# Finer rounding ladders in a quantised feed-forward layer and a fourth slope term in an attention layer

## The reference, cut to what matters

```python
# attention 0: 16 heads of 64, T = 2048, d = 1024
scores = einsum('bhqd,bhkd->bhqk', q, k) / scale
bias = -dist * slopes[:, None, None]            # slopes 2 ** (-8 h / 16)
attn = softmax(where(causal_mask, -inf, bias) + scores)
out = einsum('bhqk,bhkd->bhqd', attn, v) @ Wo.T
...
# feed-forward 1: 1024 -> 4096 -> 1024
def activation_quant(x):
    scale = 127.0 / clip(max(abs(x), axis=-1), EPS_Q, None)
    return clip(round(x * scale), -128, 127) / scale
def bitlinear(x, norm_w, w):                    # rmsnorm, quantise, product
    x_q = activation_quant(rmsnorm(x, norm_w))
    return einsum('bsd,hd->bsh', x_q, weight_quant(w))
h = bitlinear(x, norm1_w, w1)                   # x_q has 1024 columns
h = act_scale * square(relu(h)) + act_bias
y = bitlinear(h, norm2_w, w2)                   # x_q has 4096 columns
```

## Time and profile before

| what | value |
|---|---|
| time, median of 3 runs | 22603.05 us (22590.02 to 22631.4) |
| the profiled execution's own time | 22617.48 us |
| its span, slowest core (6) | 22615.7 us |
| spans of the 8 cores | 22516.5 to 22615.7 us |
| busy TensorE / VectorE / ScalarE | 7728.4 / 4516.8 / 6436.2 us (34% / 20% / 28%) |
| mean granted TensorE clock, core 6 | 0.543 |

### The profile page before, as it was taken

One profiled execution on the slowest core, in us unless ns is written; L12 is line 12 of the kernel. 1 busy time (PEld: TensorE's weight loads), 2 busy tenths in 40 slices (PEclk: granted clock), 3 DMA queues, 4 the chain that ended last, 5 costly groups with the idle time before them and its releaser, 6 DMA issues.

```text
span 22615.7 us, 119266 instructions; the slowest of 8 cores (22516.5 to 22615.7 us)
## 1 busy us (share of the span) xinstructions
PE 7728.4 (34%) x23230; PEld 2145.1 (9%) x23230; DVE 4516.8 (20%) x11318; ACT 6436.2 (28%) x12902; POOL 301.4 (1%) x487
## 2 busy tenths in 40 slices
PE   4555555555553422334433442000034200000444
PEld 1111111111111200000000000000011000000111
DVE  0011111000112221110022001113521355554000
ACT  2333333333331102444434443222333222111000
POOL 0000000000000000000000000000000000000000
PEclk6555555555555555555555555555567655555666
DMA  2000000000002211000000000111022111111222
GB/s 44 2 2 3 2 10 14 2 3 2 2 16 44 51 60 36 0 0 0 0 8 0 0 0 15 49 53 34 10 67 85 60 34 34 35 35 40 63 66 63
DMA packets 726154, 593.91 MB, mean 26 GB/s; under 512 B 438240, under 2 KB 619136, under 8 KB 725440
## 3 DMA queue, kind: packets, MB, share of 16 engines
q1 hardware_dynamic: 566272, 469.95, 6.9%
q0 software_dynamic: 159168, 116.35, 2.8%
HBM read 365.69 MB, written 201.59 MB: 25 GB/s over the span
## 4 chain that ended last, share of the span: by engine, by line
PE 28%; ACT 22%; DVE 18%; DMA 15%; issue 12%; SPq 4%; DVEq 1%; ACTq 1%; POOL 0%; POOLq 0%; PEldq 0%
SPq L213 4%; ACT f32a L1512 4%; ACT pbuf L1364 4%; PE pb L1868 3%; PE pb L726 3%; ACT pbuf L719 3%; PE pb L1370 3%; ACT pbuf L1324 3%; PE pb L702 3%; PE pb L698 3%; DMA scr<-stage_b 2%; DMA stage_b<-f32a 2%; PE pb L1347 2%; PE pb L622 2%; PE pb L626 2%
## 5 line engine op out<-in xcount | busy, mean ns | idle before, releaser
L1868 PE MATMUL pb<-wbuf,xT 128*128 128x512 bf16 x2048 | 776.2, 562 | 3994.0 <-DMA wbuf<-stage_w 3994.0
L1512 ACT ACTIVATE f32a<-scr,k_biases 128x1024 f32<-128x1024 f32 x704 | 807.8, 1147 | 2858.1 <-DVE scr L1506 2094.5
L719 ACT ACTIVATE pbuf<-pb 128x512 bf16<-128x512 f32 (+3 forms) x1280 | 682.1, 533 | 2690.4 <-PE pb L702 1432.0
L1364 ACT ACTIVATE pbuf<-pb,stat 128x512 bf16<-128x512 f32 (+3 forms) x1280 | 797.4, 623 | 1712.1 <-PE pb L1347 944.7
L1370 PE MATMUL pb<-pbuf,qk 128*128 128x512 bf16 (+3 forms) x1280 | 665.3, 520 | 1506.5 <-ACT pbuf L1364 1506.5
L726 PE MATMUL pb<-pbuf,qk 128*64 128x512 bf16 (+3 forms) x1280 | 691.9, 541 | 1231.2 <-ACT pbuf L719 1231.2
L1310 PE MATMUL pb<-qk 128*128 128x512 bf16 (+2 forms) x1280 | 637.3, 530 | 1014.4 <-ACT pbuf L1324 1011.4
L1324 ACT ACTIVATE pbuf<-pb,stat 128x512 bf16<-128x512 f32 (+2 forms) x1280 | 797.4, 623 | 549.2 <-PE pb L1310 264.3
L641 ACT ACTIVATE pbuf<-pb,stat 128x512 bf16<-128x512 f32 (+3 forms) x1280 | 797.4, 623 | 538.4 <-DVE pb L634 260.5
L622 PE MATMUL pb<-qk 64*128 64x512 bf16 (+3 forms) x1280 | 671.1, 524 | 643.2 <-ACT pbuf L641 637.1
L712 DVE TENSOR_TENSOR pb<-pb,k_zmask 128x128 f32<-128x128 f32 x512 | 153.4, 300 | 3241.5 <-PE pb L702 3241.5
(11 more groups left out here) (260 smaller groups left out, 10287.8 us busy)
## 6 DMA issues: line engine op xcount, KB each, us to landing
stage_b<-f32a SPq DMA_DIRECT2D x256, 256.0 KB, 2.4
scr<-stage_b SPq DMA_DIRECT2D x128, 512.0 KB, 3.9
wbuf<-stage_w SPq DMA_DIRECT2D x512, 128.0 KB, 2.4
stage_b<-pbuf SPq DMA_DIRECT2D x256, 128.0 KB, 1.7
wbuf<-stage_b SPq DMA_DIRECT2D x256, 128.0 KB, 2.6
f32a<-w1T POOLq DMA_DIRECT2D x128, 256.0 KB, 3.0
f32a<-w2T POOLq DMA_DIRECT2D x128, 256.0 KB, 2.9
xT<-stage_w SPq DMA_DIRECT2D x256, 128.0 KB, 3.5
```

The lines of the kernel that those rows point to most:

```text
L719: ca = p.on("act", lambda a, b=b, kt=kt, a0=a0, ph=ph: a.activation(out=ph[:, a0:512], in_=pb.t[b][:, a0:512], func=AF.Exp), inc=1)
L1364: ca = p.on("act", lambda a, b=b, a0=a0, ph=ph: a.activation(out=ph[:, a0:512], in_=pb.t[b][:, a0:512], func=AF.Exp, bias=numax), inc=1)
L1512: aw = p.on("act", lambda a, m=m, sgn=sgn: a.activation(out=sg, in_=e_, func=AF.Sign, scale=sgn, bias=self.cst["biases"][:, 260 + m:261 + m]),
L1868: t_e.matmul(pb.t[tt][:, 0:512], self.xT[:, jc * 512 + tt * 128: jc * 512 + tt * 128 + 128], w2s[j4][:, :], start=(jc == 0), stop=(jc == 31)),
```

## The change

- **Rounding in stage A.** The one call of `_round_cols` on 1024 columns becomes two calls of a new `_round_cols2` on 512 columns each. It rounds in two steps: a quarter of the source is cast to int8 and back, a ladder of range 7 (14 rungs) corrects it, the result is scaled by 4, and a second ladder of range 2 (4 rungs) corrects the remainder.
- **Rounding in stage C.** `_round_range` goes from 2 to 3, so 6 rungs for 4 in every call.
- **The exponential of pass 2 (L719)** gets a bias from a [128,1] column of the table `biases`, where it had none.
- **A fourth slope term.** The slopes are split into four bfloat16 numbers for three; the slope matmul of pass 1 has contraction 8 for 6, the tables `slopes6` and `biases` grow (264 to 272 columns), and the load of six slope rows into `crows` reads at another offset. The matmul L702 keeps contraction 8.
- **Debug probes** are added that are not built into this kernel (`debug` is False).

```diff
@@ l0 head, pass 1
-                    self.cst["slptab"][r1:r1 + 6, h * 128:(h + 1) * 128],
-                    self.cst["ramp2"][r1:r1 + 6, c * 512:c * 512 + Lc],
+                    self.cst["slptab"][r1:r1 + 8, h * 128:(h + 1) * 128],
+                    self.cst["ramp2"][r1:r1 + 8, c * 512:c * 512 + Lc],
@@ l0 head, slope rows
-                           self.cst_in["slopes6"][h * 6:h * 6 + 6, :])
+                           self.cst_in["slopes6"][h * 8:h * 8 + 6, :])
@@ l0 head, pass 2
-                    out=ph[:, a0:512], in_=pb.t[b][:, a0:512], func=AF.Exp),
+                    out=ph[:, a0:512], in_=pb.t[b][:, a0:512], func=AF.Exp,
+                    bias=self.cst["biases"][:, h * 16 + kt:h * 16 + kt + 1]),
@@ new functions
+    def _ladder(self, e_, acc, sg, nr):
+        p = self.p
+        first = True
+        for m in range(nr):
+            for sgn in (1.0, -1.0):
+                p.wait("act", "dve", p.cnt["dve"])
+                p.dep("act")
+                aw = p.on("act", lambda a, m=m, sgn=sgn: a.activation(
+                    out=sg, in_=e_, func=AF.Sign,
+                    scale=sgn, bias=self.cst["biases"][:, 260 + m:261 + m]),
+                    inc=1)
+                p.wait("dve", "act", aw)
+                p.dep("dve")
+                if first:
+                    p.on("dve", lambda v, sgn=sgn: v.tensor_scalar_mul(
+                        acc, sg, sgn), inc=1)
+                    first = False
+                elif sgn < 0:
+                    p.on("dve", lambda v: v.tensor_sub(acc, acc, sg), inc=1)
+                else:
+                    p.on("dve", lambda v: v.tensor_add(acc, acc, sg), inc=1)
+
+    def _round_cols2(self, src_ap, dst_ap, n, i8off=0):
+        p = self.p
+        i8 = self.i8t[:, i8off:i8off + n]
+        e1 = self.scr2[:, 0:n]
+        sg = self.f32a[:, 0:n]
+        acc = self.f32a[:, 512:512 + n]
+        p.dep("dve")
+        p.on("dve", lambda v: v.tensor_scalar_mul(e1, src_ap, 0.25))
+        p.dep("dve")
+        p.on("dve", lambda v: v.tensor_copy(i8, e1))
+        p.dep("dve")
+        p.on("dve", lambda v: v.tensor_copy(dst_ap, i8))
+        p.dep("dve")
+        p.on("dve", lambda v: v.tensor_sub(e1, e1, dst_ap), inc=1)
+        self._ladder(e1, acc, sg, 7)
+        p.dep("dve")
+        p.on("dve", lambda v: v.tensor_scalar_mul(dst_ap, dst_ap, 4.0))
+        p.dep("dve")
+        p.on("dve", lambda v: v.scalar_tensor_tensor(
+            out=dst_ap, in0=acc, scalar=2.0, in1=dst_ap,
+            op0=ALU.mult, op1=ALU.add))
+        p.dep("dve")
+        p.on("dve", lambda v: v.tensor_sub(e1, src_ap, dst_ap), inc=1)
+        self._ladder(e1, acc, sg, 2)
+        p.dep("dve")
+        c = p.on("dve", lambda v: v.scalar_tensor_tensor(
+            out=dst_ap, in0=acc, scalar=0.5, in1=dst_ap,
+            op0=ALU.mult, op1=ALU.add), inc=1)
+        return c
@@ l1_ffn, stage A
-            self._round_range = 3
-            c = self._round_cols(self.f32b[:, 0:1024], self.scr[:, 0:1024],
-                                 1024)
+            for kq in range(2):
+                c = self._round_cols2(self.f32b[:, kq * 512:kq * 512 + 512],
+                                      self.scr[:, kq * 512:kq * 512 + 512],
+                                      512)
@@ l1_ffn, stage C
-                    self._round_range = 2
+                    self._round_range = 3
```

More of the change, by code:

```diff
@@ L38, in make_consts @@
     s3 = bf(slopes.astype(np.float64) - s1 - s2)
-    c["_s123"] = np.stack([s1, s2, s3])
+    s4 = bf(slopes.astype(np.float64) - s1 - s2 - s3)
+    c["_s123"] = np.stack([s1, s2, s3, s4])
     ramp_m = np.zeros((128, SEQ), dtype=np.float32)
-    for i in range(3):
+    for i in range(4):
         ramp_m[2 * i, :] = ramp_m[64 + 2 * i, :] = bf(j % 256)
@@ L45, in make_consts @@
     c["ramp2"] = ramp_m
-    s6 = np.zeros((NH * 6, SEQ), dtype=np.float32)
+    s6 = np.zeros((NH * 8, SEQ), dtype=np.float32)
     for h in range(NH):
-        for i in range(3):
-            s6[h * 6 + 2 * i, :] = s6[h * 6 + 2 * i + 1, :] = (s1, s2, s3)[i][h]
+        for i in range(4):
+            s6[h * 8 + 2 * i, :] = s6[h * 8 + 2 * i + 1, :] = \
+                (s1, s2, s3, s4)[i][h]
     c["slopes6"] = s6
@@ L53, in make_consts @@
         r1 = 64 - 64 * (h % 2)
-        for i in range(3):
-            st[r1 + 2 * i, h * 128:(h + 1) * 128] = (s1, s2, s3)[i][h]
-            st[r1 + 2 * i + 1, h * 128:(h + 1) * 128] = (s1, s2, s3)[i][h]
+        for i in range(4):
+            st[r1 + 2 * i, h * 128:(h + 1) * 128] = (s1, s2, s3, s4)[i][h]
+            st[r1 + 2 * i + 1, h * 128:(h + 1) * 128] = (s1, s2, s3, s4)[i][h]
     c["slptab"] = st
@@ L82, in make_consts @@
     c["ones_row"] = np.ones((1, 128), dtype=np.float32)
-    bt = np.zeros((128, 264), dtype=np.float32)
+    bt = np.zeros((128, 272), dtype=np.float32)
     for h in range(NH):
         for kt in range(16):
-            bt[:, h * 16 + kt] = slopes_bf[h] * 128.0 * kt
+            bt[:, h * 16 + kt] = s4[h] * (128.0 * kt +
+                                          np.arange(128, dtype=np.float32))
     bt[:, 256] = 1e-5
@@ L90, in make_consts @@
     bt[:, 259] = 0.5
-    bt[:, 260] = -0.5
-    bt[:, 261] = -1.5
-    bt[:, 262] = -2.5
+    for m in range(7):
+        bt[:, 260 + m] = -0.5 - m
     c["biases"] = bt
@@ L305, in _declare_io @@
             ("tie_row", [1, SEQ]), ("ones_row", [1, 128]),
-            ("biases", [128, 264]), ("slopes6", [NH * 6, SEQ]),
+            ("biases", [128, 272]), ("slopes6", [NH * 8, SEQ]),
             ("slptab", [128, NH * 128]),
@@ L341, in _declare_io @@
             ("tie_row", [1, SEQ], BF16), ("ones_row", [1, 128], BF16),
-            ("biases", [128, 264], F32), ("qpos", [128, 16], F32),
+            ("biases", [128, 272], F32), ("qpos", [128, 16], F32),
             ("eoct", [64, 512], BF16), ("e16", [64, 512], BF16),
@@ L516, in l0_attn @@
                         self._l0_head(s, pair * 2 + h2, h2, qT, kT, vb)
+                if self.debug and s == 0 and pair == 7:
+                    p.probe(self, "qT7", qT[:, 0:SEQ], [128, SEQ], BF16)
+                    p.probe(self, "kT7", kT[:, 0:SEQ], [128, SEQ], BF16)
+                    p.probe(self, "vb7", vb[:, 0:SEQ], [128, SEQ], BF16)
+                    p.probe(self, "ctxall", self.ctxT[:, 0:8 * SEQ],
+                            [128, 8 * SEQ], BF16)
             if self.l0_stage >= 4:
@@ L535, in _l0_head @@
         s123 = _c["_s123"][:, h]
-        S3 = float(float(s123[0]) + float(s123[1]) + float(s123[2]))
+        S3 = float(float(s123[0]) + float(s123[1]) + float(s123[2]) +
+                   float(s123[3]))
         slope = S3
@@ L656, in _l0_head @@
                 carr[:, qt:qt + 1], negu[:, qt:qt + 1], lnw))
+        if self.debug and s == 0 and h == 0:
+            p.probe(self, "carr0", carr, [128, 16], F32)
         cin_even = bass.AP(self.util, 32, [[64, 128], [2, 16]])
@@ L718, in _l0_head @@
                 pb.reading(b, "act")
-                ca = p.on("act", lambda a, b=b, kt=kt, a0=a0, ph=ph: a.activation(
-                    out=ph[:, a0:512], in_=pb.t[b][:, a0:512], func=AF.Exp),
+                ca = p.on("act", lambda a, b=b, kt=kt, a0=a0, ph=ph, h=h:
+                          a.activation(
+                    out=ph[:, a0:512], in_=pb.t[b][:, a0:512], func=AF.Exp,
+                    bias=self.cst["biases"][:, h * 16 + kt:h * 16 + kt + 1]),
                     inc=1)
@@ L772, in _l0_wo @@
                 pb.read_done(b, "dve", c)
+            if self.debug and s == 0 and qt == 0:
+                p.probe(self, "pre0", self.f32a[:, 0:1024], [128, 1024], F32)
+                p.probe(self, "st0", self.stat[:, 8:10], [128, 2], F32)
             self._ln_from_f32a(s, qt, nsum=2, write_fp32_out=False, stage=True)
+            if self.debug and s == 0 and qt == 0:
+                p.probe(self, "lnout0", self.res_tile(0, 0), [128, 1024], BF16)
+                p.probe(self, "stln0", self.stat[:, 24:28], [128, 4], F32)
     def l0_ffn(self):
```

## The result

The changed kernel takes 25106.37 us, the median of 8 runs (25035.46 to 25135.23), against 22609.76 us before in 8 runs. The ratio is 1.1098 (95% interval 1.1084 to 1.1112), so it is 11% slower, within 13 us of the forecast of 25,093 us. The profiled execution took 25077.02 us, with a span of 25075.6 us on core 2.

What follows compares the result with a forecast made beforehand. Chains of instructions waiting for each other, not engines, bound stages A, C and pass 2. Stage C 693, stage A 1682 and the bias 115 sum to 2490 us on 22603.05, giving 25,093 us, range 24,950 to 25,200 us.

Steps and rivals of the forecast that it cites:

- Nothing bounds stages A and C but the chain: Stages A and C: no engine bounds them; signs and adds wait for each other, 2.707 us per rung of 1024 columns.
- Stage C, 693 us: Stage C: two more rungs per call, 256 rungs of 2.707 us, covered by nothing, add 693 us.
- Stage A, 1682 us: Stage A: 36 rungs of 512 for 6 of 1024; each of 32 tiles goes from 19.97 to 72.54 us, adding 1682 us.
- The bias, 115 us: Pass 2: the bias lengthens each of 1280 exponentials by 0.090 us, all on the chain, adding 115 us.
- The step from L641 to L719: Exponentials from PSUM: L641 with a bias takes 687 ns, L719 without one 597, so the bias costs 90 ns.
- the argument from L1512: Ladder sign L1512 waits before every rung yet takes 1147 ns, so idle time gives the pass 2 bias no discount.
- The slope term, nothing: Pass 1: contraction 8 for 6 costs nothing, as matmuls with 8 and 6 rows both take 604 ns.
- TensorE's clock in stages B and D: Stages B and D: a clock moved by the longer pause ahead, shifting matmul sums by tens of us, would contradict the prediction.
- the bias is seen in TensorE's wait: Rival for pass 2: the bias is hidden and pass 2 stays unchanged, 24,978 us in all; chance 6%.
- the handoffs at half the width: Rival for pass 2 and stage A: 0.05 us more per iteration and short pair, 25,215 us in all; chance 6%.
- the clock stays at its lower level: Rival: TensorE holds its higher clock in attention and stage D, saving 2550 us against 2490, 22,543 us in all; chance 1%.
- The overlap was priced too low: Rival for stage A: its halves overlap, adding 411 us in place of 1682, 23,822 us in all; chance 2%.

Runs made afterwards that it cites:

- the interleaved halves: The changed kernel with stage A's two halves interleaved rung by rung on tiles of their own, without self waits there, sum in bfloat16: 24069.98 us, ratio 1.0621.
- the rounding constant: The changed kernel with both ladders replaced by adding and subtracting 1.5 * 2 ** 23 in float32, bias and fourth slope term kept: 20560.39 us, ratio 0.9081.
- the kernel with two operands: The changed kernel whose pass 2 exponential also takes its scale from a [128,1] column of ones: 25279.04 us, ratio 1.116 to the kernel before.

## Why the prediction was right, point by point

- **Nothing bounds stages A and C but the chain.** Right, and shown from two sides: the interleaved halves take 1068 us out of stage A with the same steps, and the rounding constant takes 2254 and 2331 us out of A and C. In stage C the chain has links that the forecast didn't name and didn't need, the waits for loads and stores, 463.1 and 94.2 us; they stayed as they were.
- **Stage C, 693 us.** 686.1 in the changed kernel, 694.5 alone.
- **Stage A, 1682 us.** 1667.3; a tile takes 79.6 us for the 80.1 foreseen. Two terms were a little too dear. The scaling by 4, taken from the nearest row at 427 ns, takes 295, so 64 x 0.132 = 8.4 us less. With the rule of the Trainium skill ("VectorE: DVE Perf Modes", "The perf-mode tier table"), four elements a cycle, from which the forecast had estimated 0.29 us, the trace agrees. The pair of handoffs is 0.331 us for 0.335, which makes 1152 x 0.004 = 4.6 us. The casts stay at 427 ns, so the upper bound of 34 us wasn't needed.
- **The bias, 115 us.** 113 to 114 alone, 116 for each of two. The step from L641 to L719 was read rightly, and so was the argument from L1512 that a wait hides nothing. The row of the kernel with two operands shows it on the same instruction. The overlap of back-to-back activations that the Trainium skill names ("ScalarE: Activation LUTs", "What ACT_TABLE_LOAD costs") did not reach this chain, and is seen where signs do follow each other: in the interleaved kernel the second starts 0.093 us before the first ends, and the two take 1.33 us.
- **The slope term, nothing.** 0.9999, and the contraction of 8 takes 604 ns.
- **TensorE's clock in stages B and D.** Not moved: 0.78 and 0.62 on core 2, where they were 0.78 and 0.63, and stage lengths within 4 us of those before.
- **The rest, 25,093 against 25,106.** The forecast adds 2490 us; the parts that the stages show add up to 2476 us (alone) and the whole to 2497. Agreement to 13 us is in part luck, for the kernel before has medians of 22610, 22654, 22658 and 22676 us in four sets of runs. The traces show two places where time varies without the change touching them. From the end of pass 2 to the start of stage A the eleven traces need between 9023 and 9064 us, by the medians of the cores. In the kernel with the slope term alone, which has the time of before, stage A starts 45 us later than before, and 41 of them arise there. And stage B takes 1148 to 1252 us, each time nearly the same on cores 0 and 1, 2 and 3, 4 and 5, 6 and 7. In the trace of before it takes 1248.5 us on core 6 and 1150.8 on core 0, at the same granted clock (0.78), and nearly all of the difference is TensorE's wait for the loads of the weights (521.0 us for 451.0) and for ScalarE (188.7 for 159.8). The time is that of the slowest core, which in the profile of before is core 6 with its long stage B; in the profile of the changed kernel no core has one. What lengthens these loads was not tried.

The rivals fell for these reasons: the bias is seen in TensorE's wait; the handoffs at half the width are the same; the halves share `scr2`, `f32a` and `i8t`; and the clock stays at its lower level of 1.2 GHz (0.50) in stages A and C, where TensorE has next to nothing to do, and at 0.53 and 0.50 in attention 0 and 1 on core 2. The overlap was priced too low: as a kernel of its own it leaves stage A 599 us longer than before, not 411. With two halves in flight it is not VectorE that sets the pace but the rung of one half, 1.61 us, in which VectorE works 1.31.

## What to carry to other kernels

Where two engines hand a tile back and forth and neither is busy for half of the stage, an added instruction costs its own duration and its hop, each time, and the sum can be made from the rows before. Such a chain is shortened by wider instructions, by a second tile in flight, and by leaving out waits that another wait implies, in this case by 518 us, 1068 us (149 of them by the waits) and 239 us; but first ask whether the arithmetic needs the chain, for here two instructions do for a whole tile what 44 did for each half. An operand that comes from a column in place of a constant lengthens the instruction even when its engine stands idle before it.

## What the runs showed of the hardware beyond the forecast

- A second wait whose condition is already met lengthens a hop between ScalarE and VectorE by 0.05 to 0.07 us when it stands behind the wait that ends last; over 1920 rungs the stages gave back 239 us.
- Two ScalarE instructions of 721 ns back to back take 1.33 us in place of 1.44; the second starts 93 ns before the first ends.
- Stage B, in which TensorE waits for loads of weights, takes 1148 to 1252 us, alike within 10 us on the two cores of a pair (0 and 1, 2 and 3, and so on); in one trace 1248.5 and 1150.8 us at a granted clock of 0.78 both.
- Each [128,1] column operand adds 90 ns to an activation, also the second one (597, 687, 777 ns), with the engine idle for over a microsecond before it.
